# One class table, a hinge for the scale embedding, and a normalised x turned by TensorE

## The reference, cut to what matters

```python
h = _ln(x, pw_g[pathway_ids], pw_b[pathway_ids])
h = _ln(h, cp_g[compartment_ids], cp_b[compartment_ids])
t = _ln(x, tm_g[time_steps], tm_b[time_steps])
m = x + _mlp_ln(memory_state, ...)[:, None, :]     # n and r alike, with other nets
s = _ln(x, ms_g[scale_type], ms_b[scale_type])
w = jax.nn.softmax(aw)
cat = jnp.concatenate([w[0]*h, w[1]*t, w[2]*m, w[3]*n, w[4]*r, w[5]*s], axis=-1)
out = x + _ln(silu(cat @ int_W1 + int_b1) @ int_W2 + int_b2, int_g, int_be)
```

## Time and profile before

| what | value |
|---|---|
| median of three runs | 942.07 us |
| profiled execution, its span | 940.0 us, 13618 instructions |
| TensorE matmuls busy | 929.1 us, 99% of the span |
| VectorE busy | 804.7 us, 86% |
| GpSimd busy | 467.5 us, 50% |
| ScalarE busy | 276.5 us, 29% |
| granted TensorE clock, mean | 0.998 |

### The profile page before, as it was taken

How to read it: one execution, slowest core, us unless ns; L and a number is a source line. 1 busy time by engine, 2 the same in 40 slices (tenths; PEclk the granted TensorE clock), 3 DMA queues, 4 the chain that set the end, 5 groups by cost and what they waited for, 6 DMA issues and landing times.

```text
span 940.0 us, 13618 instructions
## 1 busy us (share of the span) xinstructions
PE 929.1 (99%) x4219; PEld 747.9 (80%) x4219; DVE 804.7 (86%) x1171; ACT 276.5 (29%) x353; POOL 467.5 (50%) x620
## 2 busy tenths in 40 slices
PE   8999999999999999999999999999999999999996
PEld 7677887878888787888878888787888878788785
DVE  7989998888888888888888888888888888888665
ACT  5635132241411313231241322224132131323211
POOL 3355564655446365454646446355444636545022
PEclk9999999999999999999999999999999999999999
DMA  9984776657475764856577485665747567485332
GB/s 325 358 279 146 232 172 228 165 169 230 115 235 134 244 169 133 241 148 214 147 201 207 115 241 136 229 179 148 229 137 232 136 225 187 119 236 156 83 82 66
DMA packets 98994, 174.56 MB, mean 186 GB/s; under 512 B 11552, under 2 KB 50464, under 8 KB 95008
## 3 DMA queue, kind: packets, MB, share of 16 engines
q0 software_dynamic: 22976, 66.07, 29.0%
q1 hardware_dynamic: 44032, 91.87, 28.0%
q10 hardware_dynamic: 31968, 16.39, 6.0%
HBM read 141.54 MB, written 32.75 MB: 185 GB/s over the span
## 4 chain that ended last, share of the span: by engine, by line
PE 96%; DVE 2%; DMA 1%; ACT 0%; issue 0%; POOL 0%; SPq 0%; DVEq 0%; POOLq 0%
PE hid_ps L1516 25%; PE hid_ps L1517 24%; PE hid_ps L1518 24%; PE o_ps L1617 3%; PE o_ps L1615 3%; PE made_ps L1617 3%; PE made_ps L1615 3%; PE made_ps L1616 3%; PE o_ps L1616 3%; PE made_ps L1468 1%; DMA keep<-int_W 1%; DVE w_raw L1150 1%; PE o_ps L1436 0%; PE hid_ps L1523 0%; PE o_ps L1425 0%; PE o_ps L1424 0%
## 5 line engine op out<-in xcount | busy, mean ns | idle before, releaser
L1516 PE MATMUL hid_ps<-cat_hi,w_hi 128*128 128x512 f32 x1008 | 396.7, 394 | 0.0
L1517 PE MATMUL hid_ps<-cat_lo,w_hi 128*128 128x512 f32 x1008 | 392.8, 390 | 0.0
L1518 PE MATMUL hid_ps<-cat_hi,w_lo 128*128 128x512 f32 x1008 | 392.4, 389 | 0.0
L1516 PEld LDWEIGHTS hid_ps<-cat_hi,w_hi 128*128 128x128 f32 x1008 | 189.2, 188 | 49.8 <-issue 11.1
L1518 PEld LDWEIGHTS hid_ps<-cat_hi,w_lo 128*128 128x128 f32 x1008 | 189.3, 188 | 40.1
L1517 PEld LDWEIGHTS hid_ps<-cat_lo,w_hi 128*128 128x128 f32 x1008 | 189.3, 188 | 38.2
L568 POOL DMA_INDIRECT pw_rows<-pw,path_now x64 | 90.3, 1411 | 110.6 <-DVE y_sb L1056 94.5
L776 ACT ACTIVATE cat_hi<-v_ring 128x1024 fp32r<-128x1024 f32 x64 | 66.7, 1060 | 131.9 <-issue 82.6
L575 POOL DMA_INDIRECT pw_rows<-cp,class_now x64 | 82.6, 1291 | 34.8 <-DVE y_sb L1031 17.7
L589 POOL DMA_DIRECT2D r_sb<-x x60 | 56.8, 946 | 79.9 <-DVE r_sb L1119 72.3
L802 ACT ACTIVATE z_sb<-hid_ps,batch_bias 128x512 f32<-128x512 f32 x64 | 43.9, 692 | 168.4 <-PE hid_ps L1518 168.4
(11 more groups left out here) (177 smaller groups left out, 1367.0 us busy)
## 6 DMA issues: line engine op xcount, KB each, us to landing
x_sb<-xp SPq DMA_DIRECT2D x16, 1024.0 KB, 5.2
out<-r_sb SPq DMA_DIRECT2D x63, 256.0 KB, 2.1
xc<-xT SPq DMA_DIRECT2D x15, 1024.0 KB, 8.5
h_turned<-y_sb ACTq DMA_DIRECT2D x60, 256.0 KB, 6.4
r_sb<-x POOLq DMA_DIRECT2D x60, 256.0 KB, 4.4
v_ring<-h_turned SPq DMA_DIRECT2D x60, 256.0 KB, 3.5
stats_bc<-token_stats SPq DMA_DIRECT2D x120, 64.0 KB
ids_sb<-ids SPq DMA_DIRECT2D x16, 256.0 KB, 5.2
```

The source lines that it names most:

```text
L1516: pe.matmul(acc, w1_hi[:, k, cols], hi, start=start, stop=False)
L1517: pe.matmul(acc, w1_hi[:, k, cols], lo, start=False, stop=False)
L1518: return pe.matmul(acc, w1_lo[:, k, cols], hi, start=False, stop=stop)
```

## The change

It does five things.

1. `ORDER` becomes x, t (four tiles), s (four tiles), h. A pair now holds two feature tiles of t, or two of s.
2. The scale gain is no longer picked. A gain that takes three values at kind 0, 1, 2 is a straight line plus a bend: |slope x kind + at_zero| + lift, up to a sign that is put into the weights (`side_mix`) and shifts. ScalarE makes the absolute value from `kinds_sb`, the kinds as integers on all partitions (`hinges`, four instructions a batch). VectorE adds `lift` and multiplies by x in one instruction a tile.
3. TensorE picks only the class gains: four matmuls in one round a batch, by `onehot` itself. `scaled`, `scaled_next` and `fill_more` are gone.
4. So `xc` must be the normalised x: `scale_x`, a multiplication over 128x2048, follows `centre`. The statistics are no longer split in two parts, and come back in one transfer.
5. For batch 0 ScalarE normalises x token-first (`x_norm`), TensorE turns it (`turn_x`, 16 transposes) and ScalarE copies it to `xc`. The fourteen small columns of the hinge are made once by GpSimd (`hinge_columns`).

```diff
+            def hinges(b, j):
+                act.wait_ge(kinds_in, 16 * (b + 1))
+                act.wait_ge(used, 6 * b + j - 1)
...
+                for i in range(2):
+                    f = 2 * (j - 2) + i
+                    act.activation(v_ring[:, slot(TS0 + j), i, :], kinds_sb[:, :], ACT.Abs, scale=slope[:, f:f + 1],
+                                   bias=at_zero[:, f:f + 1]).then_inc(hinged, 1)
...  ScalarE, chunk 1
+                    hinges(b, 2)
+                    hinges(b, 3)
                     ts_high(b, 2)
                     h_write(b)
                     ts_high(b, 3)
...  ScalarE, every later chunk
                     ts_high(b, 0)
                     ts_high(b, 1)
+                    hinges(b, 2)
                     h_write(b)
+                    hinges(b, 3)
                     ts_high(b, 2)
                     ts_high(b, 3)
...
+            def scale_x(b):
+                dve.wait_ge(centred, b)
+                rs = stats_bc[:, :, P:2 * P].unsqueeze(1).to_broadcast([P, FT, TT, P])
+                by_groups = xc.rearrange("q f (g j) -> q f g j", j=P)
+                dve.tensor_tensor(by_groups, by_groups, rs, ALU.mult).then_inc(xhat_done, 1)
...
             def ts_mult(b, j):
...
+                if j >= 2:
+                    dve.wait_ge(hinged, FT * b + 2 * (j - 1))
+                    for i in range(2):
+                        f = 2 * (j - 2) + i
+                        v = v_ring[:, slot(TS0 + j), i, :]
+                        ins = dve.scalar_tensor_tensor(v, v, lift[:, f:f + 1], xc[:, f, :], ALU.add, ALU.mult)
...
-                                  xc[:, j:j + 1, :].to_broadcast([P, 2, TOKENS]), ALU.mult).then_inc(v_done, 1)
+                                  xc[:, 2 * j:2 * j + 2, :], ALU.mult).then_inc(v_done, 1)
...  VectorE, the loop's chunk
                     onehot_next(b + 1)
-                if not (first or last):
-                    scaled_next(b + 1)
                 out_sum(b - 1, 2)
...
                     centre(b + 1)
+                    scale_x(b + 1)
                 out_sum(b - 1, 3)
...  TensorE
-                pick(b, 0)
-                pick(b, 1)
+                for f in range(FT):
+                    pick(b, f)
...
                 pair(b, 1)
-                fill_more(b)
...  GpSimd, x_rstd of a later batch
-                pool.tensor_copy(x_pack[:, 0, 0, :], xmv[:, :, 0]).then_inc(x_packed, 1)
-                pool.tensor_copy(x_pack[:, 1, 0, :], xmv[:, :, 0]).then_inc(x_packed, 1)
-  (and four tensor_tensor that split 1/deviation)
+                pool.tensor_copy(x_pack[:, 0, :], xmv[:, :, 0]).then_inc(x_packed, 1)
+                pool.tensor_copy(x_pack[:, 1, :], xrs[:, :]).then_inc(x_packed, 1)
...  SyncE: load_kinds(b + 1), 256 KB, behind load_ids(b + 1) and ahead of load_xT(b + 1)
+                wait(sp, hinged, FT * b)
+                sp.dma_start(kinds_sb[:, :], kinds[b].partition_broadcast(P)).then_inc(kinds_in, 16)
...  TensorE, batch 0
-                mean_first()
                 x_high_part(1)
                 x_low_part(1)
-                dev_first()
+                turn_x(0)
                 x_high_part(2)
                 first_fill(0)
                 x_low_part(2)
+                turn_x(1)
...
-                first_fill(2)
                 pair(0, 3)
-                first_fill(3)
```

More of the change, by code:

```diff
@@ L37, with build @@
 GROUP, GROUPS = 32, 4
-HALF = GROUP // 2
 CLASSES, SCALES = 5, 3
-def build(nc, x, xp, xT, ids, pid, small, small_at, tabs, rows, net_vecs, pw, cp, W1s, W2s, int_W1, int_W2, out):
+def build(nc, x, xp, xT, ids, kinds, pid, small, small_at, tabs, rows, net_vecs, pw, cp, W1s, W2s, int_W1, int_W2, out):
     f32, f32r, i32 = mybir.dt.float32, mybir.dt.float32r, mybir.dt.int32
@@ new lines, in x_rstd, with hinge_columns, step @@
+                pool.tensor_copy(x_pack[:, 1, :], xrs[:, :]).then_inc(x_packed, 1)
+            def hinge_columns():
+                steps = [0]
+                def step(out, a, b, op):
+                    steps[0] += 1
+                    pool.tensor_tensor(out, a, b, op).then_inc(hinge_step, 1)
+                    pool.wait_ge(hinge_step, steps[0])
+                low, mid, high = [s_gains[:, :, k] for k in range(SCALES)]
+                pool.wait_ge(small_in, 16)
+                step(gain_diff, high, low, ALU.subtract)
+                step(gain_half, gain_diff, c_half, ALU.mult)
+                step(gain_sum, high, low, ALU.add)
+                step(gain_mid, gain_sum, c_half, ALU.mult)
+                step(gain_bend, gain_mid, mid, ALU.subtract)
+                pool.wait_ge(signs_ready, 2)
+                step(side, gain_twice, c_one, ALU.subtract)
+                step(bend_size, side, gain_bend, ALU.mult)
+                step(slope, bend_size, half_size, ALU.add)
+                step(turned_half, side, gain_half, ALU.mult)
+                step(at_zero, turned_half, slope, ALU.subtract)
+                step(turned_mid, side, gain_mid, ALU.mult)
+                step(lift, turned_mid, slope, ALU.subtract)
+                step(s_shifts[:, :, :], shifts[:, FT:2 * FT, 0:SCALES], side.unsqueeze(2).to_broadcast([P, FT, SCALES]), ALU.mult)
+                pool.wait_ge(mix_ready, 1)
+                step(side_mix, side, w_mix[:, 5:6].to_broadcast([P, FT]), ALU.mult)
@@ L825, in _ @@
             act.activation(class_tab[:, :], class_tab[:, :].bitcast(f32), ACT.Copy, scale=tab_sign).then_inc(tab_hi_done, 1)
+            sum_high(1)
+            sum_first(2)
+            for t in range(TT):
+                x_norm(t)
             sum_high(2)
+            xhat_copy(0)
+            sum_first(3)
             nets_join()
-            sum_first(3)
             sum_high(3)
@@ L1178, in alike @@
                             shift.unsqueeze(2).to_broadcast([P, FT, GROUPS, n]))
-                for cols, at, shift in kinds:
+                mine = parts[1:2] if of_s else (parts[0], parts[2])
+                if of_s:
+                    dve.wait_ge(hinge_step, 13)
+                for cols, at, shift in mine:
                     for base in (HI, AGAIN):
@@ L1286, in first_chunk @@
                 centre(1)
-                scaled_next(1)
+                scale_x(1)
                 y_add(1, 0)
@@ L1476, in first_fill @@
                     pe.wait_ge(v_done, j)
-                pick(0, j)
+                for i in range(2):
+                    pick(0, 2 * j + i)
             def fill_and_bias(b):
-                pe.wait_ge(scaled_ready, b + 1)
                 pe.wait_ge(onehot_ready, b + 1)
```

287 lines of the change are left out of this document (136 added, 151 removed).

## The result

The changed kernel takes 952.4 us (951.2 to 952.7 in four runs), the kernel before 942.3 in the same session (941.8 to 942.9): ratio 1.0105, 95% interval [1.0093, 1.0117]. It is 10.1 us slower. I had forecast 948.0 us and a range of 937 to 956, with slower as the likeliest outcome. The profiled execution took 952.2 us, with a span of 950.5; its granted clock is 0.997, against 0.998 before.

What follows compares the result with a forecast made beforehand. TensorE bounds the kernel before at 56.00 us a batch; VectorE would bound the changed one at 56.52. Batch 15's pair 2 at 143.5 + 13 x 56.52 + 4.7 = 883.0, span 945.9, plus 2.1: 948.0 us, range 937 to 956.

Steps and rivals of the forecast that it cites:

- TensorE alone at 55.33 us: TensorE's batch period without the second pick round: 56.00 less 0.67 us.
- VectorE's way round the loop at 56.52 us: VectorE's queue followed wait by wait over one batch: shifts end at +0.52 on 56.00 us, making VectorE the bound.
- The wait at the hinge, 1.84 us: VectorE's multiplication for pair 5 idles 1.84 us for `hinges(b, 3)`, behind `h_write` in ScalarE's queue; `ts_low` j = 2 shifts +1.63.
- my lower bound: Hinge wait priced at 1.2 us with h written quickest; h issued in 3.3 us gives TensorE's period of 55.33.
- GpSimd's smaller share: `x_rstd` on GpSimd loses four of six small instructions; power ready 0.8 us earlier, so `out_sum` t = 0 shifts +0.83.
- my +0.40: VectorE's `out_sum` t = 2: shift +0.83 less 0.43 us, its GpSimd power taking 0.54 instead of 0.97.
- Output t = 3: `out_sum` t = 3 on VectorE: its old 0.52 us wait for the power is hidden; `scale_x` adds 2.29, shift +1.94.
- rival 3: `scale_x` holds up GpSimd's power, so `out_sum` t = 3 starts 0.55 us later a batch: 955 us; chance 0.13.
- The cancelled wait of 1.42 us: VectorE's 1.42 us idle before the next batch's first multiplication goes: shift +1.94 becomes +0.52.
- The entrance, batch 0 at 0 and batch 2's first multiplication at 143.5: Batch 0's changes taken as 0, between -1.5 and +1.5 us; batch 1's first multiplication at 88.5, batch 2's at 143.5.

Runs made afterwards that it cites:

- table of two by two: Changed kernel 952.4 us; with h issued from SyncE instead of ScalarE 934.8; with `scale_x` left out 933.6; with both changes 933.7.
- the late pair: Changed kernel with h issued from SyncE, and batch 0's second pair of hinges moved on ScalarE behind `ts_high` of pair 4: 933.9 us.

## Why the prediction was right, and what was off

- **TensorE alone at 55.33 us.** Right: 55.30 wherever TensorE bounds. The 0.67 for the round came as 0.70; that its four picks were the smaller part of that, I had not seen.
- **VectorE's way round the loop at 56.52 us.** Right, measured 56.59 as a mean. The table of two by two shows the mechanism: hinge wait and `scale_x` together pass TensorE's loop, each alone does not. That the size came so near is in part luck. In the batch at 487.71, with a period of 56.49, `ts_low` j = 2 stands 2.01 us later than before where I had 1.63, output t = 0 1.06 instead of 0.83, t = 2 0.62 instead of 0.40, t = 3 1.99 instead of 1.94, and the end of the loop 0.49 instead of 0.52: what the hinge took more was given back step by step. The mean then holds five batches with the long gather (batch 2 with 57.86 among them), one at 55.48, and 56.04 for batch 14.
- **The wait at the hinge, 1.84 us.** Right in its place and cause, too small: 2.0 to 2.3 in most batches. A hinge takes 804 ns where I took the 0.66 us of a pair with one operand by partition (1.32 for two): the pair is 1.52, 0.2 more. And `h_write` took 3.9 to 4.1 us. The one batch between 544.20 and 599.68 is my lower bound come true: there h took 3.03 us, the wait was 1.17 and the period 55.48.
- **GpSimd's smaller share.** Right in kind: the wait before output t = 0 is 0.47 where it was 0.61, and at t = 2, where my +0.40 came from a shorter power, the power took 0.57 us and the batches with the short gather wait 0.78. What I had as fixed and isn't is the gather ahead of that power: where it takes 3.12 us the wait is 1.79. That is the variation between 56.49 and 56.98, and a term that I didn't look for. The trace of before has it too, 3.11 us in two of its batches (those at 310.90 and 478.90), with waits of 1.13 and 0.78 at t = 2; the period stayed 56.00 there, since TensorE set it.
- **Output t = 3.** Right: no wait. The power beside `centre` started at 642.28 and took 2.51 us, to 644.79, which is 0.42 us behind `centre`'s end at 644.37 and ahead of `scale_x`'s end: rival 3 is out. The Trainium skill (SBUF — State Buffer, Who interferes with whom) says that the port pair is an exclusive lock and that issue order decides who blocks. That a step which already waits gets its turn between two of VectorE's was my inference from it; the trace agrees with the inference.
- **The cancelled wait of 1.42 us.** Right: 599.68 and 656.66 wait for nothing.
- **The entrance, batch 0 at 0 and batch 2's first multiplication at 143.5.** Wrong, and this is most of what the median is off (952.4 against 948.0): 147.31, 3.8 us later. It has two parts of like size. Batch 1's first multiplication came at 90.45 where I had 88.5. These are `centre` for batch 1 before, and `centre` and `scale_x` after:

```profile
73.63 2.29 DVE L955 TENSOR_TENSOR xc<-xc,stats_bc 128x2048 f32<-128x2048 f32 x1
```

```profile
75.57 2.27 DVE L1014 TENSOR_TENSOR xc<-xc,stats_bc 128x2048 f32<-128x2048 f32 x1
77.88 2.30 DVE L1021 TENSOR_TENSOR xc<-xc,stats_bc 128x2048 f32<-128x2048 f32 x1
```

So `scale_x` less `scaled_next` made its 1.6 us, and 1.9 came from batch 0, which I had put at 0. I had counted batch 0's changes on TensorE and on GpSimd and left out ScalarE's own four hinges, 2.93 us ahead of `ts_high` for pair 4; the late pair shows 0.9 us of that, and leaving out `x_norm` 0.4 by the medians. The rest isn't settled. Part may be the execution itself: in the version with both hinge pairs ahead of `h_write`, whose batch 0 is the same, `centre` starts at 76.16.

The other 1.9 us are in batch 1, and there my sum was wrong by itself. I put 1.62 on and took 1.06 off batch 2's old start, 142.90, as if batch 1 had begun at its old time, though I had just made it 1.6 late. The delay isn't caught up: `ts_low` for pair 5 stands at 108.48 instead of 104.78, 3.7 later. With it my terms give 88.5 + 56.00 + 1.62 - 1.06, a period of 56.56 for batch 1; measured were 56.86. That leaves 0.3. In this batch `y_mul` waits 1.24 us at 117.00 for h to be written, because `h_write` stands 3.5 us later than before (102.69 and 99.17), and with h on SyncE the period is 55.54.

- **The period's miss** of 0.07 us makes 0.9 us over 13 batches. With the entrance's 3.8 that is 4.7, against the 4.6 us by which the span was longer than forecast (950.5 and 945.9).

The faster version had been within the reading of the profile: the prediction named the place of `h_write` in ScalarE's queue as the cause of the one wait that decides. Moving it and the late hinge pair give 933.9 us, 18.5 less than the changed kernel and 8.3 less than before.

## What to carry to other kernels

When the bound engine is relieved, price the second engine's way round the loop wait by wait and not by its busy time: here two costs that alone came to 0 and 1.1 us made 18.7 together. Look in the queue of every engine that a new operand comes from for DMA instructions ahead of it; issuing four of them held ScalarE's queue for about 4 us here, which is free only until somebody waits behind them. Walk the entrance with the same care as the loop, engine by engine, since a few microseconds there are as large as a change of 0.3 us a batch, and carry a delay on into the next step of the sum.

## What the runs showed of the hardware

- A 128x512 activation with scale and bias both by partition took 804 ns on int32 input (64 of them) and 805 ns on f32 (batch 0's four `x_norm`); with a scale alone 716 ns (60 of them). The int32 input isn't what costs. The Trainium skill (ScalarE: Activation LUTs, What ACT_TABLE_LOAD costs) gives about 93 ns for each operand by partition; the difference of 88 ns agrees.
- ScalarE's queue began to issue DMAs (597.01) while its activations still ran (to 597.96), but a following activation waited for the issuing to end (601.06, 0.05 us behind it).
- GpSimd's indirect gather took 0.95 to 3.12 us for the same 256 KB. Next to `h_low` and `x_low`, VectorE instructions with two SBUF inputs, it took 1.98 or 3.12; the two gathers behind it about 1.0. Moved ahead of the power for output t = 1 it took 1.09, and the one now next to `h_low` 3.05. So the place decides; the port as the reason is not tested. What decides between 1.98 and 3.12 is open.
